# Leaving out the 44 dummy matmuls that stand in front of a Trainium2 kernel's first transposes

## The reference

```python
x = x + 0.5 * ffn(layernorm(x))
x = x + attn(layernorm(x))      # z = x W^T; h = z + sum_k eta[k] * scan(lam[k], z); gamma * norm(h) + beta
x = x + 0.5 * ffn(layernorm(x))

def ffn(x):                     # w_gate, w_up: [2048, 512], w_down: [512, 2048]
    gated = silu(einsum('bsd,hd->bsh', x, w_gate)) * einsum('bsd,hd->bsh', x, w_up)
    return einsum('bsh,dh->bsd', gated, w_down)
```

## Time and profile before

| | us |
|---|---|
| time before, median of 3 runs | 1050.61 (1050.35 to 1051.24) |
| the profiled execution's own time | 1050.32 |
| its span, first to last instruction | 1048.5 |
| PE busy | 1042.8 (99%) |
| DVE busy | 642.7 (61%) |
| ACT busy | 352.3 (34%) |
| PE's first instruction, a dummy | 1.56 |
| PE's first transpose | 9.38 |
| PE's first plain product | 12.69 |

### The profile page before, as it was taken

The page is one execution under the profiler, slowest core; times in us unless marked ns, Lnnn a source line. Parts: engine busy times, 40 slices in busy tenths (PEclk is TensorE's granted clock), DMA queues, the critical chain, the costliest instruction groups (busy, mean ns, idle before and its releaser), DMA issues.

```text
span 1048.5 us, 12846 instructions
## 1 busy us (share of the span) xinstructions
PE 1042.8 (99%) x4742; PEld 865.1 (83%) x4742; DVE 642.7 (61%) x973; ACT 352.3 (34%) x589; POOL 108.1 (10%) x127
## 2 busy tenths in 40 slices
PE   9999999999999999999999999999999999999998
PEld 8888888888888888888888888888888888888887
DVE  6855666569677657777757765787665333333342
ACT  6644544533322322222522222222243322222321
POOL 3123332110010110001002001000000000000000
PEclk9999999999999999999999999999999999999999
DMA  6588876678665555655545655555657565556256
GB/s 201 212 321 319 302 261 241 219 233 272 230 198 192 181 181 181 201 196 195 168 166 191 200 181 180 180 186 176 203 191 228 201 198 194 181 187 203 84 193 206
DMA packets 58381, 215.80 MB, mean 206 GB/s; under 512 B 6096, under 2 KB 15312, under 8 KB 50640
## 3 DMA queue, kind: packets, MB, share of 16 engines
q1 hardware_dynamic: 58176, 214.98, 60.9%
q10 hardware_dynamic: 144, 0.00, 0.0%
HBM read 170.92 MB, written 44.04 MB: 205 GB/s over the span
## 4 chain that ended last, share of the span: by engine, by line
PE 99%; DVE 1%; DMA 0%; DVEq 0%; issue 0%; SPq 0%
PE ps_a L1308 8%; PE ps_a L1310 8%; PE ps_a L1309 8%; PE ps_b L1308 8%; PE ps_b L1310 8%; PE ps_b L1309 8%; PE ps_c L1308 6%; PE ps_c L1310 6%; PE ps_c L1309 6%; PE ps_d L1308 6%; PE ps_d L1310 6%; PE ps_d L1309 6%; PE aux L1310 3%; PE aux L1308 3%; PE aux L1309 3%; PE ps_d L1508 1%
## 5 line engine op out<-in xcount | busy, mean ns | idle before, releaser
L858 DVE TENSOR_TENSOR tmp<-tmp,ps_c 128x512 f32<-128x512 f32 x59 | 40.6, 687 | 139.6 <-PE ps_c L1310 139.6
L1308 PE MATMUL ps_a<-xt,gu 128*128 128x512 f32 x304 | 119.5, 393 | 0.1
L1310 PE MATMUL ps_a<-xt,gu 128*128 128x512 f32 x304 | 118.5, 390 | 0.0
L1309 PE MATMUL ps_a<-xt,gu 128*128 128x512 f32 x304 | 118.4, 389 | 0.0
L1308 PE MATMUL ps_b<-xt,gu 128*128 128x512 f32 x286 | 111.9, 391 | 0.0
L1310 PE MATMUL ps_b<-xt,gu 128*128 128x512 f32 x286 | 111.4, 390 | 0.0
L1309 PE MATMUL ps_b<-xt,gu 128*128 128x512 f32 x286 | 111.4, 389 | 0.0
L1308 PE MATMUL ps_d<-dn,hid 128*128 128x512 f32 x256 | 100.8, 394 | 0.0
L1310 PE MATMUL ps_d<-dn,hid 128*128 128x512 f32 x256 | 99.8, 390 | 0.0
L1309 PE MATMUL ps_d<-dn,hid 128*128 128x512 f32 x256 | 99.7, 390 | 0.0
L1308 PE MATMUL ps_c<-xt,gu 128*128 128x512 f32 x236 | 92.1, 390 | 0.0
(11 more groups left out here) (204 smaller groups left out, 2032.9 us busy)
## 6 DMA issues: line engine op xcount, KB each, us to landing
dn<-dn_kept SPq DMA_DIRECT2D x112, 512.0 KB, 3.3
gu<-gu_kept SPq DMA_DIRECT2D x46, 1024.0 KB, 5.1
gu<-gu_kept SPq DMA_DIRECT2D x46, 768.0 KB, 5.4
gu_kept<-gu SPq DMA_DIRECT2D x14, 1024.0 KB, 4.5
gu_kept<-gu SPq DMA_DIRECT2D x14, 768.0 KB, 4.2
dn_kept<-dn SPq DMA_DIRECT2D x16, 512.0 KB, 5.1
zw<-zw_kept SPq DMA_DIRECT2D x16, 512.0 KB, 3.3
h_t<-w_ffn_in SPq DMA_DIRECT2D x18, 256.0 KB, 4.7
```

The source lines that it names most:

```text
L858: dve.tensor_tensor(dst, u3s(si), p5_bank(si)[:, :], ALU.add).then_inc(c22_done, 1)
L1308: pe.matmul(dst, a_hi, b_hi, start=start, stop=False, skip_group_check=chained)
L1309: pe.matmul(dst, a_hi, b_lo, start=False, stop=False, skip_group_check=chained)
L1310: return pe.matmul(dst, a_lo, b_hi, start=False, stop=stop, skip_group_check=chained)
```

## The change

The constant `WARM` and the one call that used it are taken out. The wait for `ident` stays, and so do the four dummy matmuls (in records of the trace) behind the second turn and the ten behind the fourth. Nothing else is touched, and no other engine's list changes.

```diff
-    WARM = 22
     KEEP = {1: 2, 3: 5}
@@
             pe.wait_ge(ident_ready, 1)
-            keep_warm(WARM)
             for r in range(4):
                 turn_x(0, r)
                 if r in KEEP:
                     keep_warm(KEEP[r])
```

## The result

The changed kernel takes 1052.84 us (median of 12 runs, 1052.06 to 1054.45), the kernel before, run beside it, 1050.53 us (12 runs, 1050.20 to 1052.12). The ratio is 1.0023, with a 95% interval of 1.0015 to 1.0031: 2.3 us slower. The forecast was 1053.2 us, in a range of 1051.6 to 1055.2, with 0.60 for slower by over 0.2%; the interval lies around that bound, so the direction is clear, and whether the size is above 0.2% is not.

What follows compares the result with a forecast made beforehand. PE was taken as the bound from the first transpose at 9.38 us. Removed dummies cost 0; 5.3 us of slow pace at 0.48 adds 2.55 us to 1050.61, giving 1053.2 us, range 1051.6 to 1055.2.

Steps and rivals of the forecast that it cites:

- The dummies' own price, 0: Before the first transpose: removing 44 matmuls, 6.88 us of PE off the path, gains 0 by itself.
- 0.48 us for each slow microsecond: Behind 9.38 us: each microsecond PE stays at 0.214 us per matmul instead of 0.111 costs 0.48 us.
- The lag: How long PE stays slow from 9.38 us: 3.6 to 7.0 us, costing 1.7 to 3.3 us; chance 0.52.
- The middle of 5.3 us: Slow time taken from the first transpose, with the jump at 14.7 us: a loss of 2.55 us.
- The lower end: From the first transpose: slow for 3.6 us, as in the trace, jump at 13.0 us, loss 1.7 us.
- The upper end, 7.0 us: From the first transpose: 16 transposes bring the jump no nearer, so it comes at 16.4 us, loss 3.3 us.
- Nobody new waits: Behind the turns: PE gets no new wait; it reaches the second four tiles with 2.5 us left.
- What gives it back: Behind 9.38 us: only a stall not hanging on PE could; at most 0.2 us, at 44.4 us.
- The short lag: Rival at the first turns: jump after 2 to 3.6 us, loss 1.0 to 1.7 us; chance 0.13.
- Transposes don't raise the clock: Rival at the first turns: jump 3.6 us behind the last transpose, 17.5 us, loss 3.8 us; chance 0.23.
- the slow pace belongs to the program's first 5 us: Rival at the start: slow pace isn't from PE's idleness, transposes run fast, 1050.3 to 1050.6 us; chance 0.09.
- Same or slower: Whole kernel, against a bound of 0.2% (2.1 us): slower 0.60, same 0.37, faster 0.03.

Runs made afterwards that it cites:

- warm_nokeep: The kernel before, 44 front dummies kept, without the four dummies between the turns and the ten behind them: 1050.10 us against 1050.53, ratio 0.9998.
- again1: The changed kernel profiled once more with no edit: 1054.13 us, against 1052.06 us in its first profile.
- turns_first: The kernel before with its 44 front dummies replaced by 44 transposes of the identity: 1050.50 us against 1050.41, ratio 1.000.
- late9: The kernel before with 18 dummies, run once the first rows of x have landed, in place of 44 from 1.56 us: 1050.74 us against 1050.41, ratio 1.0001.

## Why the prediction was right, and where it was not

The sign, the size and the mechanism came out: 2.3 us more (2.55 forecast), lost by PE's slow pace in front of the first plain products, and kept to the end. That the size is so near is in part luck, as the lag below shows: the four measured lags have a mean of 4.5 us, which by 0.47 gives 2.1 us, and the late transfer adds its own spread to the times.

- **The dummies' own price, 0.** Right: 44 matmuls less, and nothing came sooner. PE still waits for DVE's row. It holds as long as the dummies end before the first transpose can start: they did by 0.95 us at a lag of 3.6 us, and by 0.20 us at 5.5 us (warm_nokeep).
- **0.48 us for each slow microsecond.** Right: 0.47 in four profiles of the same program. The slow price of transposes is 0.214 us (eight take 1.71 us in again1) and that of plain products 1.9 times the fast one; both had been taken over from the dummies.
- **The lag.** The middle of 5.3 us was a fair value (3.1, 3.7, 5.6, 5.6 measured), but both of its reasons were weak. The lower end was the one lag that the trace had, 3.6 us, and I counted shorter ones only to the rival; the changed kernel's own profile has 3.1. The upper end, 7.0 us, rested on transposes that "bring the jump no nearer", and the run of transposes alone refutes that. What replaces it: the lag differs from execution to execution of the same program, from 3.1 to 5.6 us in four profiles. It had to be priced as a spread and not as one value between two mechanisms.
- **Nobody new waits.** Right at the start. In again1 the fourth turn is through at 13.87 us (13.9 forecast), and PE goes on to the plain products without a wait. PE has one wait in the whole profile of the changed kernel, for the first row, and the distance to the kernel before changes by 0.1 us from 14.3 us to the end.
- **What gives it back.** Nothing did, as said. What I left out is the opposite: the late transfer between 250 and 262 us, worth up to 1.3 us in some executions, with dummies in front as well as without. The earlier trace rows show no such wait of PE; the trace of before has it with 0.2 us in the weight loads only, which I passed over.
- **The rivals.** The short lag is not a rival but one end of the spread (3.1 us is in it, 3.7 us just outside). "Transposes don't raise the clock" has fallen by turns_first, and so has "the slow pace belongs to the program's first 5 us", by late9. The granted clock of 1.00, which spoke for the latter, was a missing record.
- **Same or slower.** The measured 0.23% stands almost on the bound of 0.2%, as the 0.37 against 0.60 had it.

## What to carry to other kernels

In this kernel TensorE is the bound and idle only at the start, waiting for its first data; work that nobody needs was free there and bought the full clock, and without it the kernel paid about half of the first 3 to 6 us of real work. Such filler should last long enough for the clock to come up in most executions, reach near to the first real instruction, and not beyond it: 16 dummies that ended 4 us early bought nothing that can be told, and 18 that ended 0.25 us before it bought about all. The lag has to be taken from several profiles, as a spread. When a column and the pace of equal instructions disagree, count the instructions: in these traces a clock column of 1.00 ahead of its first record means nothing.

## What had not been expected of the hardware

- The time from TensorE's first instruction to the full clock varies between executions of one program: 3.1, 3.7, 5.6 and 5.6 us in the changed kernel, 3.6 to 5.5 us in the five profiles that start on dummies or on transposes in their place (3.6, 3.9, 4.0, 5.1, 5.5), and 3.7, 7.9 and 8.0 us without any dummies, where a pause of 0.67 us begins 3.7 us behind the first transpose.
- Float32 transposes alone raise the clock (5.1 us behind the first one).
- A pause of 4.0 us, begun about when the clock came up, was enough to lose it again: 1.00 at 5.5 us, 0.50 from 8.9 us on; the pause of 0.9 us in the kernel before wasn't.
- A stall of up to 1.3 us between 250 and 262 us, on the fetch of the down weights, comes and goes between executions, and is as large as half of the effect under study.
